# Gated cross-attention and mixture-of-experts layer: the rows of score maxima are stored from ScalarE's queue instead of SP's

## What is computed

```python
x = x + tanh(g_xattn) * attention(layernorm(x), ctx, ctx)   # 16 heads, softmax over 128 keys
x = x + tanh(g_ffn) * experts(layernorm(x))                 # top 2 gates, the later expert's result is kept
# inside attention
scores = einsum('bhqd,bhkd->bhqk', Q, K) / sqrt(8)
attn = softmax(scores, axis=-1)
out = einsum('bhqk,bhkd->bhqd', attn, V)
```

## Time and profile before

| | |
|---|---|
| runs | 3, median 197.22 us (196.46 to 199.26) |
| the profiled execution | 196.55 us, of which the span is 194.7 us |
| PE, DVE, ACT busy | 70%, 62%, 49% of the span |
| POOL busy, PE weight loads | 47%, 55% |
| store of the maxima | 16 issues of 8 KB |
| fills of the stacks | 48 transfers of 128 KB |
| expert weights | 8 loads of 514 KB |

### The profile page before, as it was taken

One profiled execution on the slowest core, in us unless ns is written; L12 is line 12 of the kernel. 1 busy time (PEld: TensorE's weight loads), 2 busy tenths in 40 slices (PEclk: granted clock), 3 DMA queues, 4 the chain that ended last, 5 costly groups with the idle time before them and its releaser, 6 DMA issues. The chain is left out here.

```text
span 194.7 us, 5177 instructions
## 1 busy us (share of the span) xinstructions
PE 136.3 (70%) x1646; PEld 106.8 (55%) x1646; DVE 121.2 (62%) x433; ACT 95.7 (49%) x237; POOL 91.1 (47%) x164
## 2 busy tenths in 40 slices
PE   7486549989997777289687284106987999999400
PEld 2145535667675555156465253006976999999300
DVE  5467376666698799627988067878546576665200
ACT  3227205637765665413546342055866687876100
POOL 8372885382263202405223821644415565665652
PEclk9969955979999999955889759655999999999955
DMA  5899933333325356637824140013123321001000
GB/s 166 276 280 226 222 96 86 82 88 81 89 57 141 82 142 166 197 133 201 276 85 151 52 125 5 30 47 76 45 65 103 103 73 50 23 24 43 27 0 0
DMA packets 18354, 20.53 MB, mean 105 GB/s; under 512 B 3012, under 2 KB 15815, under 8 KB 18132
## 3 DMA queue, kind: packets, MB, share of 16 engines
q1 hardware_dynamic: 16216, 16.96, 32.4%
q0 software_dynamic: 1248, 2.23, 3.5%
q10 hardware_dynamic: 864, 1.01, 1.6%
HBM read 10.88 MB, written 3.35 MB: 73 GB/s over the span
## 5 line engine op out<-in xcount | busy, mean ns | idle before, releaser
L701 DVE TENSOR_REDUCE smax<-pair 128x8 f32<-128x1024 f32 x32 | 38.6, 1212 | 12.0 <-PE pair L1003 11.9
L552 ACT ACTIVATE probs<-pair 128x1024 f32<-128x1024 f32 x32 | 32.4, 1013 | 16.8 <-PE pair L1015 16.7
L485 POOL DMA_INDIRECT out<-k_stack,token x23 | 23.1, 1006 | 24.0 <-DVE k_stack L897 15.2
L610 ACT ACTIVATE k_stack<-pair,q_stack 128x128 f32<-128x128 f32 x74 | 21.7, 370 | 12.1 <-PE pair L1107 6.7
L1107 PE MATMUL pair<-q_stack 128*128 128x128 f32 x184 | 25.6, 285 | 0.8 <-DVE q_stack L882 0.8
L1107 PEld LDWEIGHTS pair<-q_stack 128*128 128x128 f32 x184 | 23.7, 201 | 1.0 <-ACT q_stack L604 1.0
L1015 PE MATMUL pair<-q_stack,k_stack 64*128 64x128 bf16 x256 | 14.5, 241 | 12.1 <-DMA q_stack<-nmaxT 9.9
L436 POOL CAST nmax<-smax 128x16 bf16<-128x16 f32 x16 | 3.2, 198 | 40.5 <-DVE smax L701 40.5
L422 POOL DMA_INDIRECT rows_dram<-routed,rowpos x16 | 16.1, 1007 | 12.1 <-DVE rowpos L773 8.1
L1047 PE MATMUL bank<-probs,vall 128*18 128x128 f32 x512 | 21.3, 319 | 0.6 <-ACT probs L552 0.6
L1015 PEld LDWEIGHTS pair<-q_stack,k_stack 64*128 64x128 bf16 x256 | 8.2, 102 | 18.1 <-DMA q_stack<-nmaxT 14.2
(11 more groups left out here) (171 smaller groups left out, 262.0 us busy)
## 6 DMA issues: line engine op xcount, KB each, us to landing
wexp<-in_wexp SPq DMA_DIRECT2D x8, 514.0 KB
k_stack<-k_part SPq DMA_DIRECT2D x24, 128.0 KB, 3.3
q_stack<-q_part SPq DMA_DIRECT2D x24, 128.0 KB, 2.6
q_stack<-rows_dram SPq DMA_DIRECT2D x23, 72.0 KB, 1.8
x<-in_x SPq DMA_DIRECT2D x4, 256.0 KB, 8.0
ctxT<-in_ctxT SPq DMA_DIRECT2D x3, 256.0 KB, 9.4
q_stack<-in_zeros SPq DMA_DIRECT2D x6, 128.0 KB, 4.4
rows_dram<-late_pack SPq DMA_DIRECT2D x1, 576.0 KB, 5.2
```

What stands on the lines that cost most here:

```text
L485: pool.indirect_dma_start(io["out"], bass.IndirectOffsetOnAxis(ap=token[:, t:t + 1].bitcast(u32), axis=0), result[t], None, bounds_check=T ...
L552: A(probs[s % 2][:, t].rearrange("p h g q -> p (h g q)"), pairs[home["shifted", s, t]][:, :], ACT.Exp, scale=HD ** -0.5).then_inc(s_exp, 1)
L610: ins = A(hidT[t % R][:, c, :], bank[1 + t % 2][:, c * P:(c + 1) * P], ACT.Relu, bias=w1cur[t % R][:, HID + c:HID + c + 1])
L701: V.reduce_max(smax[q % 2][:, :, CHUNK * t:CHUNK * (t + 1)], pairs[home["score", q, t]][:, :].rearrange("p (h g k) -> p h g k", h=2, g=CHU ...
```

## The change

The store is taken out of SP's loop and put behind the copy on ACT. SP still waits for the copy in each turn, and then goes on with fills and loads. ACT now waits for its own copy, issues the store, and only then goes on to headsT and the second exponent. The semaphores and buffers stay.

```diff
             for m in range(SEQS):
-                c, u = seq_of(m)
                 sp.wait_ge(s_mtc, m + 1)
-                sp.dma_start(qst[6:P:32, c, :, u], nmaxT[m % 2][:, :]).then_inc(s_mrow[m % 4], 16)
                 if m in later:
                     later[m]()
...
                     A(nmaxT[m % 2][:, :], max_turned, ACT.Copy).then_inc(s_mtc, 1)
+                    act.wait_ge(s_mtc, m + 1)
+                    act.dma_start(qst[6:P:32, m // CHUNK, :, tok(m % CHUNK)], nmaxT[m % 2][:, :]).then_inc(s_mrow[m % 4], 16)
                 if h is not None:
                     wait(act, s_wo, h)
                     A(headsT[:, :], heads_turned, ACT.Identity, bias=bv).then_inc(s_htc, 1)
```

## The result

The changed kernel takes 208.9 us (median of 4 runs, 205.74 to 214.51); the kernel before, run beside it, 196.84 us. The ratio is 1.050 with a 95% interval of 1.031 to 1.070: slower, and outside the range of 195.8 to 202.5. The profiled execution is the slowest of the four (214.51 us; the others took 205.74, 208.67 and 209.13), so it is read here for what waits for what and for single latencies, not for its total. Executions of one kernel fall into a faster and a slower group some per cent apart, and the ratios leave slower ones out where they can; the ratio of the medians of all runs (1.061 here) stands beside them where it says something else.

The account below looks back on a forecast made before the run. The prediction took the store's 1.76 us landing to be on the path, with air on ACT in most steps. Terms -0.3 + 0 + 0.3 + 0.73 + 0.53 + 0.8 - 0.2 gave +1.9 us, forecast 198.7 us, range 195.8 to 202.5.

Parts of the forecast that it names:

- the store and SP's next transfer start together: In 8 waits, store and fill leave at once and meet in the DMA engines: 0.1 us each, +0.8 in all.
- The rival of colliding issues: SP and ACT issue at the same moment, ACT's issue 0.63 us longer, ten places: +6.3, 204.7 us; chance 0.15.
- The store's own start: Store on ACT issued 0.28 us after the copy's start and landing 1.76 later, as on SP: 0.
- ACT's queue, late steps: headsT and the second exponent 0.73 us later, mostly covered by air: 0.3 us for nine late steps together.
- The air of 0.14 us: Late steps: the delayed second exponent ends at 65.67, L1003 needs it at 65.81, leaving 0.14 us.
- Step 4: ACT has no air before K's cast and the chain to PE's V projection, late by the full shift: +0.73 us.
- Step 6: Gate products L940 stand behind L1084, which waits for headsT, and end after L1015's former start: +0.53 us.
- Earlier fills: SP's fills start 0.61 us earlier, shortening PE's wait for the fourth chunk's zero rows: -0.3 us.
- Stores free of SP's queue: Two late stores no longer stand behind SP's loads; the first is hidden, the second gives 0 to 0.53: -0.2 us.
- between the weight packets at once: Late store at the weight load: by the page's rule it gets in at once, gaining the whole 0.53 us.

Follow-up runs that it names:

- The separated kernels: Changed kernel, SP also waiting for headsT from the fourth turn (199.54 us), or that plus waiting for the store's landing in the first three turns (199.53 us).
- one extra copy: Kernel before, with one extra ACT copy of 128x512 elements, never read, behind each copy of the maxima: 196.27 us, ratio 0.999.
- two: Kernel before, with two extra ACT copies of 128x512 elements, never read, behind each copy of the maxima: 202.48 us, ratio 1.036.
- the first kernel with SP later: Changed kernel, but from the fourth turn on SP also waits for headsT before issuing its fill or load: 199.54 us, ratio 1.014.
- the loads later: Changed kernel, but only in the last five turns SP also waits for headsT before its issues: 202.19 us, ratio 1.029.
- the loads in pieces: Changed kernel, with the expert weight load of turns 11 to 15 in four pieces of 32 rows: 205.05 us, ratio 1.036.

## Why the prediction was wrong

- **The step that failed** is "the store and SP's next transfer start together". It was taken at 0.1 us in 8 waits, +0.8 in all, with a bound of 0.53 each. Measured: 0.53 to 0.68 behind a fill, 1.4 behind constant rows and 1.2 to 2.1 behind a load, in eleven of sixteen turns, and nothing in the other five: 12.8 us of landings in sum. The bound came from a row that doesn't show the case: the store of the earlier trace rows was issued when the loads ahead of it had been under way for some time. The case had to be bounded by how long one transfer of SP takes to pass, since both engines are released by one signal and nothing said which goes first. The separated kernels show the mechanism by its removal (from 5.0% to 1.4 and 2.0%; from 6.1 to 1.6 and 0.5 by the medians), and the load issued first on SP's queue shows it alone.
- **The rival of colliding issues** had the sign, the trigger (one signal releases both) and, by luck, with 204.7 us nearly the size, but not the place: it had ACT's issue grow to 1.06 us. Only the first did, all others took about 0.55:

```profile
L576 ACTq DMA_DIRECT2D q_stack<-nmaxT x16: 530/545/1292, 30.9 to 124.8; - x16
```

  Its point of decision, an issue over 0.71 us, would have read as "no collision". The delay lies behind the issue.
- **The store's own start**: 0.28 us, right in all but the first of the 16 turns (0.30).
- **ACT's queue, late steps**: headsT was put 0.73 us later. It is 0.88 behind the copy in place of 0.16, so 0.72. The air of 0.14 us was not reached, since the late store moved L1003 back too. That air of this order exists is borne out by one extra copy (nothing) and two (3.6%, or 2.0% by the medians).
- **Step 4**, +0.73: L503 starts 2.05 us after its step's copy (46.72) in place of 1.41 before, +0.64, and the chain behind it is as long as before: right, a little high. **Step 6**, +0.53: the projection is late as worked out, but the store lands later still, so the term was swallowed by the one that failed.
- **Earlier fills**, -0.3: the wait for the zero rows fell by 0.42 us, within 0 to 0.61, and copy to scores by 0.66: right in kind, a little low. **Stores free of SP's queue**, -0.2: nothing of it came; the store of turn 12 took 3.46 us in place of 2.24.
- The terms other than the failed one sum to 1.1 us. The kernels with the turns kept apart cost 1.4 and 2.0%, some 3 to 4 us (1 to 3 by the medians), though their fills start later than in either kernel. How much of that is ACT's lateness at 0.72 us stays open.
- **What the prediction left out** is the clock. The mean granted clock fell along with the change (0.842 to between 0.75 and 0.81). In the profiled execution part of that isn't the change's doing: the stretch ahead of the first store, where the kernels are alike, already ran at 0.75 in place of 0.86 and took 2.2 us longer. From the first store to the last it is 93.9 us in place of 82.3, at 0.74 in place of 0.85; of the 11.6 us more, PE is busy for 10.0 (73.0 in place of 62.9) and idle for 1.5 (20.9 in place of 19.4). So much of what the late landings cost shows as slower work of PE and not as waits. The kernel with the load first bears out that late landings bring the clock down; how the 12 us divide between the two stays open, as no run held the clock fixed.

The Trainium skill's rule that starting a transfer elsewhere saves only the issuing sequencer's time ("DMA: Bandwidth & Descriptors", section "Issuing engines are not separate DMA queues") points the right way: nothing was won (a ratio of 1.050), and the price was that two transfers became simultaneous.

The same page of the Trainium skill, section "Queues, rings and completion order", has an engine drain a whole packet of one row, some 9 to 17 descriptors, before it turns to the next row. The prediction, in its remark on this rule, let the store in "between the weight packets at once", as if a packet were a single piece of a transfer. In the records of this trace a load is 128 pieces of 4112 bytes and 16 semaphore writes, so 8 pieces and one write for each of 16 engines, and by the page's figure, an estimate, one turn can take all of them. The trace agrees so far: 435 to 537 KB went ahead of the store in the changed kernel, and 125 to 217 KB when the load was split. It doesn't show turns being taken beyond that: in turn 12 of the first kernel with SP later, 986 KB of two of SP's transfers, the rest of the spare rows and nearly all of a load, went ahead of ACT's store, whose first piece started 2.88 us after its issue.

## What to carry to other kernels

A small transfer whose landing is waited for must be issued ahead of any large one that the same signal releases, or apart from it: one queue in program order gives that for nothing, two queues lost it here in eleven turns of sixteen. When an issue moves to another engine, look at what the old engine does in that moment, and price the meeting by the time that transfer takes to pass. Transfers that depend on nothing late, like the constant rows here, belong where their queue is idle.

## What the runs showed of the hardware

The packet records of the trace show where the delay lies. Alone, the store's first packet (256 bytes, 32 of them) starts 1.2 us after the issue and its last 0.16 us later. Behind a fill the first starts at 1.72, and 112 to 130 KB of other packets, about one fill, have gone ahead; behind a load at 2.6 to 2.9, with 435 to 537 KB ahead, about one load; behind a quarter of a load at 1.5 to 1.7. In each case the store's own packets then pass nearly as quickly as alone, in 0.13 to 0.4 us: it is not slowed, it starts late. Whether it is held in the DMA engines' queues or before them, where the packets are made, no run separates.

Which of two transfers goes first is not settled by which issue starts first. SP's started 4 or 5 ns ahead in 46 turns of four kernels (the changed one, the loads later, the loads in pieces, and the first three turns of SP later). In the 30 in which SP's issue was over 14 ns or more before ACT's, SP's transfer went first and the store was late. In the 16 in which it was over at most 12 ns before ACT's, or after it, the store's packets went first, at 1.18 us as if alone. A load's issue lasts 0.31 to 0.34 us against the store's 0.53 to 0.56, and loads went first each time; a fill's or that of constant rows lasts 0.53 to 0.57, and they went either way. This is what the records show; no run was made to test it.

An instruction of ACT behind its own transfer started 0.60 us after that transfer's issue began (71.35 - 70.75): the issue holds up what stands behind it on ACT for its 0.55 us.
